# A tanh recurrence inside a saturated pipeline: its steps move from TensorE to VectorE and ScalarE

## The reference

```python
xB = jnp.einsum('bsd,dn->sbn', x, B)          # 256 features -> 16
h0 = jnp.zeros((8, 16))
def step(h, xb_t):
    h = jnp.tanh(xb_t + h @ A.T)              # A is 16 x 16
    return (h, h)
_, hs = jax.lax.scan(step, h0, xB)            # 1024 steps, each needs the one before
y = jnp.einsum('sbn,nd->bsd', hs, C)          # 16 -> 256
return y @ W_out.T + b_out                    # folded: C @ W_out.T is one 16 x 256 matrix
```

## Time and profile before

| | |
|---|---|
| median of the runs (three: 1692.9, 1695.86, 1700.84) | 1695.86 us |
| span of the profiled execution | 1692.7 us |
| TensorE busy, products / weight loads | 1591.6 us (94%) / 1324.5 us (78%) |
| VectorE busy | 1274.3 us (75%) |
| ScalarE busy | 1051.2 us (62%) |
| GpSimd busy | 823.1 us (49%) |
| granted TensorE clock, mean | 0.974 |
| chain that ended last | PE 82%, DVE 6%, DMA 3%, ACT 2% |

### The profile page before, as it was taken

The page is one execution under the profiler, slowest core; times in us unless marked ns, Lnnn a source line. Parts: engine busy times, 40 slices in busy tenths (PEclk is TensorE's granted clock), DMA queues, the critical chain, the costliest instruction groups (busy, mean ns, idle before and its releaser), DMA issues.

```text
span 1692.7 us, 51627 instructions
## 1 busy us (share of the span) xinstructions
PE 1591.6 (94%) x16840; PEld 1324.5 (78%) x16840; DVE 1274.3 (75%) x4556; ACT 1051.2 (62%) x3851; POOL 823.1 (49%) x1294
## 2 busy tenths in 40 slices
PE   4588999999999999999999999999999999998866
PEld 3477888888888888888888888888888888887654
DVE  4566777887788778787888787887888877876544
ACT  4656666666766666666666666666666667655431
POOL 3554454554555455545454554454545545543211
PEclk7799999999999999999999999999999999999978
DMA  5211111111111111011111111111111111110000
GB/s 151 84 57 45 52 58 58 42 39 43 43 56 56 56 51 43 31 52 47 56 56 56 46 42 35 50 50 56 56 56 43 37 44 44 52 52 8 7 7 13
DMA packets 117250, 81.49 MB, mean 48 GB/s; under 512 B 42016, under 2 KB 108224, under 8 KB 117056
## 3 DMA queue, kind: packets, MB, share of 16 engines
q1 hardware_dynamic: 116208, 80.10, 15.4%
q10 hardware_dynamic: 976, 0.54, 0.1%
HBM read 47.06 MB, written 33.55 MB: 48 GB/s over the span
## 4 chain that ended last, share of the span: by engine, by line
PE 82%; DVE 6%; issue 3%; DMA 3%; ACT 2%; SPq 2%; POOL 1%; ACTq 0%; DVEq 0%; POOLq 0%
PE ps L1254 62%; PE ps L1260 4%; PE ps L1271 4%; PE ps L1285 2%; PE ps L1301 2%; PE ps L1442 2%; PE ps L1331 2%; DMA xag<-in_x 2%; PE ps L1321 2%; PE ps L1312 1%; DVE hs L858 1%; DVE att L947 1%; DVE dstate L1075 1%; PE ps L1292 1%; DMA arow<-att 1%
## 5 line engine op out<-in xcount | busy, mean ns | idle before, releaser
L1254 PE MATMUL ps<-we,yT 128*128 128x512 f32 x3072 | 824.5, 411 | 0.3 <-DVE h2Ts L953 0.3
L1254 PEld LDWEIGHTS ps<-we,yT 128*128 128x128 f32 x3072 | 546.5, 191 | 100.9 <-issue 1.1
L566 ACT ACTIVATE h_lead<-ps 48x8 fp32r<-48x8 f32 x1024 | 172.4, 168 | 443.8 <-PE ps L1271 430.3
L858 DVE SCALAR_TENSOR_TENSOR hs<-ps,cst,h_lead 48x8 fp32r<-48x8 f32 x1024 | 224.7, 219 | 223.8 <-ACT ps L567 216.1
L1271 PEld LDWEIGHTS ps<-hs,aT 128*128 128x128 f32 x1024 | 195.1, 191 | 126.4 <-DVE hs L858 99.1
L1271 PE MATMUL ps<-hs,aT 128*128 128x8 f32 x1024 | 215.9, 211 | 39.7 <-DVE hs L858 38.3
L890 DVE SCALAR_TENSOR_TENSOR stage<-ps,coef,stage 128x256 f32<-128x256 f32 x384 | 183.1, 477 | 13.8 <-POOL stage L433 5.0
L890 DVE SCALAR_TENSOR_TENSOR acc<-ps,coef,acc 128x256 f32<-128x256 f32 x384 | 181.7, 473 | 6.6 <-POOL acc L433 2.7
L518 POOL TENSOR_TENSOR orstd<-omean,mhalf 128x32 f32<-128x32 f32 x32 | 174.6, 5455 | 0.2
L567 ACT ACTIVATE ps<-ps 48x8 f32<-48x8 f32 x1024 | 162.8, 159 | 0.0
L431 POOL TENSOR_TENSOR part<-part 128x256 f32<-128x256 f32 x64 | 46.9, 732 | 204.2 <-ACT part L584 201.8
(11 more groups left out here) (184 smaller groups left out, 3200.4 us busy)
## 6 DMA issues: line engine op xcount, KB each, us to landing
arow<-att SPq DMA_DIRECT2D x32, 512.0 KB, 2.8
atx<-arow SPq DMA_DIRECT2D x128, 128.0 KB, 2.8
vrow<-vtok SPq DMA_DIRECT2D x32, 256.0 KB, 2.1
vx<-vrow SPq DMA_DIRECT2D x128, 64.0 KB, 2.0
out<-stage SPq DMA_DIRECT2D x64, 128.0 KB
xin<-in_x SPq DMA_DIRECT2D x62, 128.0 KB
xag<-in_x SPq DMA_DIRECT2D x62, 128.0 KB
stage<-in_experts SPq DMA_DIRECT2D x1, 2048.0 KB, 9.5
```

The costliest lines, as they stand in the source:

```text
L566: a.activation(h_lead[:], ps[0:NB, BANK["RB"], k * B:(k + 1) * B], ACT.Tanh)
L858: v.scalar_tensor_tensor(hs[0:NB, :, k], h_whole, keeps_rest, h_lead[:].bitcast(F32), ALU.mult, ALU.subtract).then_inc(sem("rnn_h"), 1)
L1254: ins = t.matmul(dst, left(lp, c), right(rp, c), start=(n == 1), stop=(n == 3 * chunks))
```

## The change

TensorE no longer takes part in a step. The state of all batches and features is now one column of 128 partitions (batch times 16 plus feature), `hs[:, k]`. One step is:

1. VectorE turns blocks of 32x32: from the column, read 32 times over, to `h_row`, in which each partition has the 32 values of its pair of batches (`spread_state`).
2. VectorE multiplies with `a_by_out` (A, laid out so that the other batch of the pair meets zeros) and sums over the 32 columns into `sum_h`, 128x1 (`sum_state`), as a rule behind the operation that follows the turn in its order.
3. ScalarE takes tanh of `sum_h` with the step's input `u[:, k]` as bias and writes `hs[:, k]` (`state_of`), one instruction instead of two.

The inputs of 32 steps come to `inputs` in bank 3, 128x32, by 16 small products, and ScalarE copies them to `u` (`keep_inputs`), after `mask_queries(3)` and ahead of state 0. The read-out is 8 products, one for each batch, on 32 rows and 32 columns of the array, 256 columns wide, in banks 4 and 5; all in fp32. The bias goes to GpSimd, which makes `x2b` by one addition. Attention's output, so far in one bank, lies in two halves in banks 4 and 5.

```diff
-    "G1_7": 7, "TR": 3, "RB": 5, "RO": 4, "T2": 0, ...
+    "G1_7": 7, "TR": 3, "RB": 3, "RO": 4, "T2": 0, ...
-    3: [("G2_3", 7, ...), ("TR", 5, 'yrT'), ("SD", 2, 'dstate'), ...
+    3: [("G2_3", 7, ...), ("TR", 5, 'yrT'), ("RB", 5, 'u'), ("SD", 2, 'dstate'), ...
-    5: [("RB", 5, ("rnn_h", TS, TS))],
+    5: [("RO", 6, 'mv_m2'), ("O", 2, 'onorm')],
...
+        hs, u = sb("hs", [P, TS]), sb("u", [P, TS])
+        h_row, a_h, sum_h = sb("h_row", [P, PAIR]), sb("a_h", [P, PAIR]), sb("sum_h", [P, 1])
...
@@ GpSimd, behind rstd(mv_f, rf, "f", c3), ahead of start_acc(m1, 0, c4)
+                    pool.wait_ge(sem("x3"), past(c5 - 1))
+                    pool.wait_ge(sem("pads_zero"), 1)
+                    pool.wait_ge(sem("mv_r"), target)
+                    g.tensor_tensor(x2b[:], m1.acc[:], bout[:].unsqueeze(1).broadcast_to([P, TILES, D]), ALU.add).then_inc(sem("x2b"), 1)
...
@@ ScalarE
             def state_of(k, count):
-                act.wait_ge(sem("rnn_mm"), past((count - 1) * TS + k + 1))
-                a.activation(h_lead[:], ps[0:NB, BANK["RB"], k * B:(k + 1) * B], ACT.Tanh)
-                a.activation(h_whole, ps[0:NB, BANK["RB"], k * B:(k + 1) * B], ACT.Tanh).then_inc(sem("rnn_tanh"), 1)
+                if k == 0:
+                    act.wait_ge(sem("u"), count)
+                    act.wait_ge(sem("RO"), past(count - 1))
+                act.wait_ge(sem("rnn_sum"), past((count - 1) * TS + k + 1))
+                a.activation(hs[:, k:k + 1], sum_h[:], ACT.Tanh, bias=u[:, k:k + 1]).then_inc(sem("rnn_tanh"), 1)
+            def keep_inputs(count):
+                act.wait_ge(sem("RB"), count)
+                act.wait_ge(sem("rnn_tanh"), past((count - 1) * TS))
+                a.activation(u[:], inputs, ACT.Copy).then_inc(sem("u"), 1)
...
@@ VectorE
-            def split_state(k, count):
-                dve.wait_ge(sem("rnn_tanh"), past((count - 1) * TS + k + 1))
-                v.scalar_tensor_tensor(hs[0:NB, :, k], h_whole, keeps_rest, h_lead[:].bitcast(F32), ALU.mult, ALU.subtract).then_inc(sem("rnn_h"), 1)
+            def spread_state(k, count):
+                dve.wait_ge(sem("rnn_tanh"), past((count - 1) * TS + k))
+                last = (k - 1) % TS
+                v.transpose(h_row[:], hs[:, last:last + 1].broadcast_to([P, PAIR])).then_inc(sem("rnn_row"), 1)
+            def sum_state(k, count):
+                dve.wait_ge(sem("rnn_row"), past((count - 1) * TS + k + 1))
+                v.tensor_tensor_reduce(a_h[:], a_by_out[:], h_row[:], 1.0, 0.0, ALU.mult, ALU.add, sum_h[:]).then_inc(sem("rnn_sum"), 1)
...
@@ VectorE, in body(it): each split_state(k) becomes spread_state(k + 1), and sum_state(k + 1) comes one operation later
                 if live(it, 5):
-                    split_state(8, c5)
+                    spread_state(9, c5)
                 if live(it, 7):
                     dve.wait_ge(sem("moe2"), c7 * GROUPS)
                     combine(m2, 7, 0, BANK["G2_7"], c7)
+                if live(it, 5):
+                    sum_state(9, c5)
...
@@ TensorE: every step(k, ...) is gone; in the place of the old projection and read-out
+            def project_inputs():
+                for c in range(KC):
+                    for half in range(2):
+                        for pair in range(B // 2):
+                            b = 2 * pair + half
+                            ins = t.matmul(ps[PAIR * pair:PAIR * (pair + 1), RB, 0:TS], bin_[:, c, (1 - half) * N:(3 - half) * N],
+                                           yrT[:, c, b * TS:(b + 1) * TS], start=(c == 0 and half == 0), stop=(c == KC - 1 and half == 1),
+                                           skip_group_check=True)
+            def read_out():
+                for b in (0, 2, 4, 6, 1, 3, 5, 7):
+                    r = slice(b // 2 * PAIR, (b // 2 + 1) * PAIR)
+                    ins = t.matmul(ps[b % BQ * TS:(b % BQ + 1) * TS, RO + b // BQ, 0:D], hs[r, :], cw[r, b % 2, :], start=True, stop=True)
...
```

More of the change, by code:

```diff
@@ L89, in constants @@
     c[:, C_RESET:C_RESET + TOK] = (np.arange(TOK)[None] % TS) != 0
[L90 to L93, removed]
+    for half in range(2):
+        c[:, C_PART + half] = (p // N) % 2 == half
     return c
@@ L118, in build @@
         reset = cst[:, C_RESET:C_RESET + TOK]
-        keeps_rest, lead_sign, whole_sign = (cst[0:NB, C_PART + n:C_PART + n + 1] for n in range(3))
+        of_half = [cst[:, C_PART + half:C_PART + half + 1] for half in range(2)]
         stage = sb("stage", [P, KC * E * D])
@@ L1267, in moe @@
                 return product(ps[:, bank, :], lambda p, c: m.yT[:, p, c, i * P:(i + 1) * P], right, KC)
[L1269 to L1278 removed]
+            def project_inputs():
+                for c in range(KC):
+                    for half in range(2):
+                        for pair in range(B // 2):
[3 more added lines that the diff above has]
+                                           skip_group_check=True)
+                return ins
+            def read_out():
+                for b in (0, 2, 4, 6, 1, 3, 5, 7):
+                    r = slice(b // 2 * PAIR, (b // 2 + 1) * PAIR)
+                    ins = t.matmul(ps[b % BQ * TS:(b % BQ + 1) * TS, RO + b // BQ, 0:D], hs[r, :], cw[r, b % 2, :], start=True, stop=True)
+                return ins
             def logits(m, bank):
@@ L1329, in attend @@
                     for q in range(BQ):
-                        b, o = i * BQ + q, i * D + j * HQ * DV
-                        ins = t.matmul(ps[q * 32:q * 32 + 32, BANK["O"], o:o + HQ * DV], atx[:, b, j * TS:(j + 1) * TS],
-                                       vx[:, b, :, j * DV:(j + 1) * DV], start=(first and i == 0 and j == 0), stop=(j == J - 1),
+                        b, o = i * BQ + q, j * HQ * DV
+                        ins = t.matmul(ps[q * 32:q * 32 + 32, BANK["O"] + i, o:o + HQ * DV], atx[:, b, j * TS:(j + 1) * TS],
+                                       vx[:, b, :, j * DV:(j + 1) * DV], start=(first and j == 0), stop=(j == J - 1),
                                        skip_group_check=True)
@@ L1475, in body @@
                     ins.then_inc(sem("F2"), 1)
-                if live(it, 5):
-                    step(2, c5)
                 if live(it, 2):
@@ L1491, in body @@
                     read_state(1)
-                if live(it, 5):
-                    step(4, c5)
                 if live(it, 2):
@@ L1511, in body @@
                     ins.then_inc(sem("WO"), 1)
-                if live(it, 5):
-                    step(7, c5)
                 if live(it, 4):
@@ L1584, in body @@
                 if live(it, 2):
-                    attend(1, False).then_inc(sem("O11"), 1)
-                if live(it, 5):
-                    step(15, c5)
+                    attend(1, isinstance(it, int) and it == 2).then_inc(sem("O11"), 1)
                 if live(it, 4):
```

300 lines of the change are left out of this document (142 added, 158 removed).

## The result

| | before | after |
|---|---|---|
| median, same chip | 1694.38 us | 1885.14 us |
| ratio, 95% interval | | 1.111 [1.109, 1.114] |
| steady round, mean of 18 | 48.64 us | 56.01 us |
| busy per round: TensorE, VectorE, ScalarE, GpSimd | 48.4, 39.2, 32.4, 25.5 | 48.0, 47.0, 33.8, 26.7 |

The account below looks back on a forecast made before the run. TensorE bounds the kernel before (48.37 of 48.60 us a round); VectorE was to become the bound at 43.4 + 4.5 = 47.9 us. 32 x (48.6 - 47.9) = 22 us off 1695.9 gives 1674 us, range 1585 to 1760.

Parts of the forecast that it names:

- signs of being wrong: TensorE without a hole; a separate record after each sum with a round over 48.6; turn or sum over 0.25 us.
- I take 0.15 for product and total: VectorE's product and sum in each step: 0.15 us, beside 0.11 for the turn, so 0.26 a step.
- Queues and loads do not change in a steady round: Queues and loads in steady rounds: no change, so no time was added for them.
- TensorE alone would then need 43.9: TensorE's round: 48.6 less 4.7 us for the steps gone, with new projection and read-out taken as 0.
- Rival A: TensorE stays the bound, VectorE's waits hide, a step costs 0.16 us: 1546 us; chance 0.14, including times up to 1630.
- VectorE's round: 43.4 + 4.5: VectorE's steady round after the change: 43.4 us busy plus 4.5 us of waits, 47.9 us, above TensorE's need.
- Its waits, 4.5: VectorE's waits a round: 0.8, 0.9 and 1.4 us for states, 1.4 for logarithm and rstd.
- Logarithm and rstd: VectorE's waits for ScalarE's logarithm (0.9) and GpSimd's rstd (0.5) stay: 1.4 us a round.
- by its own bounds [...] 1630 to 1710: Time range of the sum, given for a step of 0.22 to 0.30 us and waits of 3.5 to 5.5.
- nothing for the end: Output-bias copy moved from ScalarE to GpSimd: 1.3 us within GpSimd's 23 us of idle, no effect on total time.
- Rival B: VectorE-ScalarE loop slower than the old one, total as its own instruction, step 0.30, round 50.3: 1750 us; chance 0.34.
- chances: Probabilities given: faster 0.52 (the forecast itself 0.38), same within 8.5 us 0.14, slower 0.34.

Follow-up runs that it names:

- f3: e4 with the tanh of a constant, so ScalarE does not wait for the sum; VectorE keeps all turns and sums: 1696.78 us.
- e4: Changed kernel with A in its own PSUM bank, read-out as 8 products over 128 rows, and VectorE's 39 iterations written out: 1744.51 us.
- g3: Kernel before without TensorE's step product; tanh and split stay: 1614.78 us.
- e5: Changed kernel without turn, sum and ScalarE's wait for the sum: 1616.94 us.
- e2: Changed kernel with VectorE's 39 iterations written out, nothing else: 1842.84 us.
- e3: Changed kernel with A in its own PSUM bank; attention's output and read-out in one bank, read-out as 8 products over 128 rows: 1820.37 us.
- e9: e4 with the x2b copy back on ScalarE and the output bias added by two one-row products on TensorE: 1743.63 us.
- e1: Changed kernel with the sum as a plain one-input reduction, the product with A left out: 1739.37 us.
- f1: Kernel before with 140 already satisfied waits at the end of VectorE's loop body: 2049.71 us.
- f2: e4 with the input as the sum's initial value instead of the tanh's bias: 1765.72 us.

## Why the prediction was wrong, point by point

Per steady round, each row the difference of two runs (those of f3 and e4 hold 0.4 us of TensorE's read-out that the other rows do not have):

| | us | round |
|---|---|---|
| before | | 48.64 |
| TensorE's products gone (g3; e5 the same) | -1.6 to -1.7 | 47.02 |
| turn and sum on VectorE, with their waits for ScalarE's order (f3) | +2.4 | 49.43 |
| tanh waits for the sum (e4) | +1.3 | 50.71 |
| P and F together (after) | +5.3 | 56.01 |

Two of the prediction's own signs of being wrong came: a record of its own follows each sum with a round over 48.6, and the sum lasts over 0.25 us in the mean. The steps of it that failed:

- **"I take 0.15 for product and total"** failed. The start-to-start distances were right: 0.13 for the turn (944.13, 944.26), 0.11 for product and total (944.46 and 944.57 in the same trace), 0.24 where 0.26 stood. What failed is that the price was taken as the same beside every GpSimd operation; the held ones add 3.8 us of records a round. It is the larger of the two terms: taking it away from e2 brings 3.5 us a round.
- **"Queues and loads do not change in a steady round"** failed: VectorE's body grew by 64 recorded instructions and its branch costs 2.8 us, with 0.6 further on. Taking it away from e3 brings 2.9 us a round.
- **"TensorE alone would then need 43.9"** failed: 47.0. Two thirds of the 3.1 us are waits of TensorE that the trace of before did not show, since steps filled them; the rest is the step's 0.11 us instead of 0.147. Rival A's 1546 was therefore out of reach: with no steps on TensorE and VectorE the kernel still takes 1617 (e5).
- **"VectorE's round: 43.4 + 4.5".** The need of 43.4 held where P is gone: 774.03 / 18 = 43.0 in e4.
- **Its waits, 4.5,** were 50.71 - 43.0 = 7.7. The waits for states seem to have held, 51.8 / 18 = 2.9 against 3.1, but by luck: they lie at six turns instead of thirteen, turn 25 has 1.27 us where 0.4 was put for the lack of cover, and 28 and 30 have 0.4 each where 0.7 was put. Logarithm and rstd held, 1.6 against 1.4. Missing were GpSimd's partial sum (22.2 / 18 = 1.2), a transpose (0.4), and 1.3 us in gaps of at most 0.12 us. So 47.9 was 2.8 low in a kernel with neither P nor F, and the sign was already wrong there.
- **"by its own bounds [...] 1630 to 1710"** does not follow from them: a step of 0.22 with waits of 3.5 gives 1600, a step of 0.30 with waits of 5.5 gives 1747. The sum was less sure of "faster" than it looked, since 1696 is no change.
- **x2b on GpSimd, "nothing for the end"**: it holds VectorE's second y1 (L884, 1.37 us instead of 0.40) in 30 of 32 rounds. In the time that hardly shows: e9, with the copy back on ScalarE and the bias on TensorE, is 1 us faster than e4.
- **Rival B** had the right sign and nearly e4's time (1750 and 1744.5), for half of its reason: the loop's price is there, but the separate record of the total, its other half, costs VectorE no time; it costs by the length of the body alone (e1). The measured 1885 is no success of B's: P and F are missing in it too. That there is such a record is what the Trainium skill, VectorE: DVE Perf Modes, "Two Vector instructions with no wait between them", says, and the trace agrees (L861, x1024).
- The **chances** treated the unknown as small shifts of known terms. Both large causes were terms that the sum did not have.

## What to carry to other kernels

- Ahead of putting many short operations on VectorE, split the durations of its present groups by what GpSimd does beside them; a group with two lengths tells who is held and by whom. A place in PSUM for its second input freed the short operation here.
- Count the instructions of a loop body that an edit lengthens, and look at the instruction queue: a fetch at every branch shows as "issue" on the first instruction behind it.
- Look also at what stands ahead of a short operation in its own engine's order: three wide ones made the longest wait for a state, and it stood in the trace of before.
- An engine without holes hides what it would wait for. Its pace without a part of its work is not its busy time less that part; here only 1.7 of 3.6 us came back.

## What I had not expected of the hardware

- The accumulator's record starts together with the next operation (910.17 both; so in 739 of the 1024): 0.08 us of record, nothing of time.
- A per-partition operand costs the product-sum 0.06 us (0.183 to 0.243) and the 128x1 tanh 0.09 (0.200 to 0.292).
- A satisfied wait still costs VectorE's sequencer 0.098 us for each instruction that carries two.
- TensorE's granted clock in steady rounds: 1.00 in before, e5 and g3, 0.98 in e4, 0.95 in the change, 0.93 in f1. Idle time in sum does not tell it: f2, with 5.2 us of it a round, has 1.00, and e4, with 4.3, has 0.98. Why, the runs do not show.
